# A fused attention and ternary-FFN kernel whose engine queues are written out in another order

## What is computed

```
h = concat(tok(x), txt)                                  # 16 x 165 x 256
h = h + attn(layernorm(h))
h = h + ffn(layernorm(h))

attn: q 16 heads, k and v 4 heads, head size 16, rotary embedding,
      scores masked to |i - j| <= 32, softmax, context, output projection
ffn:  act_quant(x) @ ternary(w1).T -> depthwise conv over 3 tokens + bias
      -> silu -> act_quant @ ternary(w2).T
act_quant: scale = 127 / max|row|, round, divide;  ternary(w): round(w / mean|w|) to -1, 0, 1
```

## Time and profile before

| | before |
|---|---|
| median of 3 runs | 406.79 us (406.76 to 406.89) |
| the profiled execution | 403.69 us |
| its span, first to last instruction | 401.9 us |
| PE busy | 343.6 us, 86% |
| DVE busy | 292.0 us, 73% |
| ACT busy | 258.2 us, 64% |
| POOL busy | 243.6 us, 61% |
| granted TensorE clock, mean share of full | 0.956 |

### The profile page before, as it was taken

How to read it: one execution, slowest core, us unless ns; L and a number is a source line. 1 busy time by engine, 2 the same in 40 slices (tenths; PEclk the granted TensorE clock), 3 DMA queues, 4 the chain that set the end, 5 groups by cost and what they waited for, 6 DMA issues and landing times.

```text
span 401.9 us, 8246 instructions
## 1 busy us (share of the span) xinstructions
PE 343.6 (86%) x2910; PEld 268.7 (67%) x2910; DVE 292.0 (73%) x629; ACT 258.2 (64%) x481; POOL 243.6 (61%) x240
## 2 busy tenths in 40 slices
PE   1588999899999999999999999999979989927435
PEld 1366667677777688868986788688758757716324
DVE  2256437943669888887789568889887988898961
ACT  3232455876768778877886778869667687626630
POOL 3418098099898993999699937983740661520500
PEclk9999899999999999999999999999999999977756
DMA  7682241000110100020002001100110100100011
GB/s 233 170 166 50 74 173 24 1 12 16 28 30 20 33 0 13 15 61 10 10 18 56 17 17 40 36 2 18 33 44 1 35 2 0 36 0 2 1 34 34
DMA packets 20228, 15.71 MB, mean 39 GB/s; under 512 B 11013, under 2 KB 19138, under 8 KB 20187
## 3 DMA queue, kind: packets, MB, share of 16 engines
q1 hardware_dynamic: 19292, 14.02, 13.5%
q10 hardware_dynamic: 895, 1.16, 1.1%
HBM read 7.91 MB, written 2.70 MB: 26 GB/s over the span
## 4 chain that ended last, share of the span: by engine, by line
PE 56%; DVE 14%; POOL 12%; ACT 6%; issue 5%; DMA 4%; SPq 1%; ACTq 0%; POOLq 0%; DVEq 0%
PE bank L1671 6%; PE bank L1763 5%; PE bank L1686 5%; PE bank L1591 4%; PE bank L1713 4%; PE bank L1739 4%; POOL shared L990 4%; PE bank L1643 3%; PE bank L1740 3%; PE bank L1662 3%; PE bank L1538 3%; PE bank L1654 2%; DMA cst<-in_consts 2%; PE bank L1704 2%; POOL shared L998 2%
## 5 line engine op out<-in xcount | busy, mean ns | idle before, releaser
L1333 DVE TENSOR_REDUCE mx<-bank 120x4 fp32r<-120x376 f32 (+3 forms) x88 | 44.6, 510 | 39.4 <-PE bank L1654 38.8
L1110 ACT COPY pT<-bank 94x480 f32<-94x480 f32 (+3 forms) x88 | 48.6, 556 | 18.9 <-PE bank L1671 17.5
L1671 PE MATMUL bank<-cst,pr 120*94 120x120 f32 (+3 forms) x352 | 50.6, 268 | 2.0 <-ACT pr L1101 1.8
L1101 ACT ACTIVATE pr<-bank 120x376 f32<-120x376 f32 (+3 forms) x88 | 39.8, 456 | 18.6 <-PE bank L1662 18.0
L1739 PE MATMUL bank<-xT_hi,w1T 128*128 128x330 f32 x128 | 45.5, 361 | 3.3 <-DVE xT_lo L1401 1.8
L1671 PEld LDWEIGHTS bank<-cst,pr 120*94 120x94 f32 (+3 forms) x352 | 36.8, 121 | 9.0 <-ACT pr L1101 4.4
L1740 PE MATMUL bank<-xT_lo,w1T 128*128 128x330 f32 x128 | 40.4, 320 | 0.0
L1763 PE MATMUL bank<-w2T,shared 128*110 128x256 bf16 x192 | 29.8, 309 | 9.6 <-ACT shared L1168 7.7
L1643 PE MATMUL bank<-kbd,q_hl 128*120 128x376 f32 (+3 forms) x88 | 34.5, 392 | 2.8 <-ACT pT L1110 2.3
L1662 PE MATMUL bank<-mx,neg_id 120*120 120x376 f32 (+3 forms) x88 | 34.2, 394 | 2.8 <-DVE mx L1333 2.7
L1654 PE MATMUL bank<-kbd,q_hl 128*120 128x376 f32 (+3 forms) x88 | 36.1, 411 | 0.0
(11 more groups left out here) (134 smaller groups left out, 901.5 us busy)
## 6 DMA issues: line engine op xcount, KB each, us to landing
out<-h SPq DMA_DIRECT2D x8, 330.0 KB
wn<-in_w SPq DMA_DIRECT2D x2, 1024.0 KB, 6.8
kbd<-kT SPq DMA_DIRECT2D x96, 20.6 KB, 1.9
shared<-in_x SPq DMA_DIRECT2D x4, 432.0 KB
h<-in_txt SPq DMA_DIRECT2D x1, 770.0 KB
...
```

The costliest lines, as they stand in the source:

```text
L1110: nc.scalar.copy(pT[0:cnt, g % 3, :], S_BANKS[g % 2][0:cnt, 0:HKV * QP]).then_inc(p_kept, 1)
L1333: nc.vector.tensor_reduce(mx[:, g % 4, :].bitcast(F32R), S_BANKS[g % 2][0:QP, 0:HKV * KEYS[j][1]].rearrange("p (k c) -> p k c", k=HKV), ax ...
L1671: o = nc.tensor.transpose(S_BANKS[g % 2][0:cnt, kv * QP:(kv + 1) * QP], pr[:, g % 3, kv * cnt:(kv + 1) * cnt], ident[0:QP, 0:QP])
```

## The change

The numbers of ORDER and ONCE change; no operation, buffer or wait does. On PE the same 624 operations come in another order, most of them moved by one to six places. A piece of the diff (three of its tables):

```diff
     'pe.scores': (
...
-        (373, 375, 385, 390, 399, 411, 420, 424, 429, 437, 439),
-        (447, 451, 465, 469, 479, 480, 489, 494, 499, 507, 510),
+        (373, 376, 384, 389, 400, 411, 413, 424, 428, 435, 438),
+        (446, 453, 459, 468, 478, 483, 487, 493, 499, 507, 513),
...
     'sp.place_k': (
-        (None,), (None,), (7,), (10,), (13,), (16,), (19,), (22,),
+        (None,), (None,), (8,), (10,), (12,), (14,), (18,), (22,),
     ),
...
     'sp.store': (
-        (12,), (15,), (18,), (21,), (23,), (24,), (25,), (26,),
+        (15,), (16,), (19,), (21,), (23,), (24,), (25,), (26,),
     ),
```

More of the change, by code:

```diff
@@ L129 @@
         (3, 4),
[L130 to L136, removed]
+        (19, 21),
+        (78, 80),
+        (126, 129),
+        (179, 182),
+        (248, 251),
+        (328, 334),
+        (396, 401),
     ),
@@ L139 @@
         (6, 7, 9),
[L140 to L146, removed]
+        (23, 30, 40),
+        (82, 86, 91),
+        (135, 143, 151),
+        (185, 190, 197),
+        (255, 262, 267),
+        (339, 343, 347),
+        (408, 417, 425),
     ),
@@ L149 @@
         (11, 12, 13),
[L150 to L156, removed]
+        (47, 57, 67),
+        (99, 108, 120),
+        (158, 169, 173),
+        (214, 223, 235),
+        (289, 301, 313),
+        (359, 371, 386),
+        (441, 451, 475),
     ),
@@ L212 @@
[L212 to L216, removed]
+        (42, 65, 89),
+        (114, 136, 149),
+        (187, 210, 237),
+        (265, 288, 315),
+        (342, 364, 383),
+        (415, 442, 467),
+        (489, 511, 534),
+        (557, 583, 599),
     ),
     'pe.select': (
[L219 to L224, removed]
@@ L225 @@
-        (495, 517, 538),
-        (564, 589, 601),
+        (48, 71, 92),
+        (121, 140, 157),
+        (191, 221, 239),
+        (270, 293, 322),
+        (344, 368, 388),
+        (422, 457, 471),
+        (495, 514, 543),
+        (563, 588, 601),
     ),
     'pe.out_proj': (
[L229 to L236, removed]
+        (51, 75, 95),
@@ L237 @@
+        (127, 145, 165),
+        (203, 227, 243),
+        (276, 296, 325),
+        (351, 380, 392),
+        (429, 462, 481),
+        (501, 516, 545),
+        (576, 591, 602),
     ),
     'pe.turn_xs': (
-        (146,), (203,), (286,), (389,), (438,), (511,), (571,), (603,),
+        (148,), (200,), (285,), (377,), (432,), (512,), (572,), (603,),
     ),
     'pe.up': (
[8 rows of a table removed]
[8 rows of a table added]
     ),
     'pe.turn_max': (
-        (206,), (276,), (353,), (442,), (502,), (565,), (610,), (617,),
+        (208,), (273,), (350,), (439,), (504,), (566,), (608,), (617,),
@@ L253 @@
     ),
     'pe.spread': (
-        (216,), (284,), (357,), (453,), (506,), (569,), (612,), (618,),
+        (217,), (283,), (356,), (450,), (509,), (569,), (611,), (618,),
     ),
     'pe.down': (
[L258 to L263, removed]
+        (234, 241, 252),
+        (304, 311, 332),
+        (382, 403, 418),
+        (472, 479, 490),
+        (519, 530, 538),
+        (579, 585, 592),
@@ L268 @@
         (6, 7),
[L269 to L272, removed]
+        (18, 20),
+        (54, 55),
+        (88, 89),
+        (126, 128),
         (175, 178),
-        (229, 232),
-        (274, 280),
+        (232, 235),
+        (276, 278),
     ),
     'act.keep_qk': (
[L278 to L285, removed]
+        (8, 10, 11),
+        (22, 30, 35),
+        (58, 61, 68),
+        (94, 99, 103),
+        (132, 136, 140),
+        (183, 187, 195),
+        (239, 242, 246),
+        (287, 292, 304),
     ),
     'act.keep_q': (
[L288 to L295, removed]
+        (14, 15, 16),
+        (39, 43, 49),
+        (72, 81, 83),
+        (111, 118, 122),
+        (151, 158, 166),
+        (204, 214, 221),
+        (256, 266, 269),
+        (309, 315, 338),
     ),
     'act.keep_k': (
-        (14, None),
-        (49, 51),
-        (85, None),
+        (17, None),
+        (50, 52),
+        (86, None),
         (124, None),
[L302 to L305, removed]
+        (171, None),
+        (228, None),
+        (273, None),
+        (348, None),
     ),
     'act.exp': (
[8 rows of a table removed]
[8 rows of a table added]
     ),
     'act.keep_p': (
[8 rows of a table removed]
[8 rows of a table added]
     ),
     'act.keep_ctx': (
-        (32, 45, 58),
-        (78, 92, 103),
-        (128, 147, 159),
+        (31, 45, 62),
+        (77, 91, 101),
+        (129, 146, 164),
         (186, 198, 217),
         (238, 253, 264),
-        (287, 306, 318),
-        (340, 354, 365),
+        (286, 307, 323),
+        (339, 352, 365),
         (385, 402, 414),
@@ L337 @@
     'act.keep_sel': (
[L338 to L345, removed]
+        (38, 51, 66),
+        (84, 96, 108),
+        (143, 155, 169),
+        (191, 205, 226),
+        (245, 260, 270),
+        (299, 319, 329),
+        (347, 358, 378),
+        (396, 408, 417),
     ),
     'act.quant_x': (
-        (93,), (134,), (189,), (248,), (288,), (350,), (391,), (None,),
+        (93,), (135,), (189,), (248,), (289,), (350,), (391,), (None,),
     ),
     'act.high_x': (
-        (100,), (144,), (200,), (271,), (307,), (357,), (397,), (420,),
+        (102,), (144,), (200,), (267,), (306,), (356,), (397,), (420,),
     ),
     'act.mid': (
[8 rows of a table removed]
[8 rows of a table added]
     ),
@@ L365 @@
         (167, 181),
-        (219, 236),
+        (218, 236),
         (284, 297),
-        (327, 342),
-        (373, 383),
+        (324, 341),
+        (372, 383),
         (410, 419),
@@ L373 @@
     'act.conv_g': (
-        (156, 160),
-        (204, 208),
+        (157, 159),
+        (202, 208),
         (254, 261),
-        (322, 326),
-        (355, 358),
+        (322, 327),
+        (357, 359),
         (398, 399),
-        (431, 432),
+        (430, 432),
         (436, 437),
@@ L397 @@
         (20, 29, 39),
-        (48, 54, 61),
+        (47, 54, 58),
         (79, 90, 101),
-        (119, 128, 142),
-        (154, 165, 172),
-        (189, 203, 216),
-        (227, 241, 252),
+        (118, 128, 142),
+        (155, 165, 171),
+        (189, 202, 214),
+        (228, 239, 252),
         (266, 282, 290),
@@ L435 @@
     'dve.silu': (
-        (71, 80),
+        (70, 80),
         (None, 114),
@@ L471 @@
     'dve.add_ffn': (
-        (102, 112, 115),
-        (136, 143, 156),
-        (171, 182, 188),
-        (218, 224, 229),
-        (243, 251, 256),
-        (278, 284, 286),
+        (103, 107, 115),
+        (136, 145, 156),
+        (175, 183, 191),
+        (218, 222, 230),
+        (244, 251, 256),
+        (278, 285, 287),
         (313, 316, 318),
```

99 lines of the change are left out of this document (48 added, 51 removed), and 154 rows, old and new, of the table ORDER.

## The result

| | before | after |
|---|---|---|
| median | 405.58 us of 20 runs (403.67 to 407.84) | 408.35 us of 20 runs (404.75 to 412.26) |
| ratio after to before, 95% interval | | 1.0053, 1.0028 to 1.0077 |
| the profiled execution | 403.69 us | 404.76 us |
| its span | 401.9 us | 403.0 us |
| PE busy | 343.6 us | 342.7 us |

The changed kernel is slower by 0.53%, about 2.1 us. The medians of the table differ by 2.8 us; they include two slow runs of the changed kernel (411.44 and 412.26 us), which the ratio leaves out. Forecast were 407.9 us and "slower by 0.2% to 0.7%". Sign and size came out; the sum that led there did not, as the trace shows at once.

A forecast was written before the change was run, and what follows sets the result against it. PE's own work bounds the kernel from 48 to 353 us, so reordering wins at most 16 us of idle time. Terms 1.7 + 0.2 - 0.8 - 0.4 - 0.4 + 0.4 + 0.4 = +1.1 us; median 407.9 us, range 404.4 to 411.2.

The forecast's parts named there:

- The forecast case: Whole kernel slower by 0.2% to 0.7%, likeliest 407.6 to 409.6 us; chance 0.33.
- start: 0 to 48 us: 0; if the cover is gone, one DVE copy of about 1 us is paid.
- pair 0: 48 to 80 us: +0.2 us, as turn_k(1,0) loses its 0.6 us of cover, for +0.4.
- single hops: 80 to 285 us: hops with under 0.6 us of PE work between their ends go from 5 to 13; +1.7 us.
- turn_xs(4): PE's 0.83 us wait near 255 us goes because POOL runs dequant_x(4) before rope(7,0); -0.8 us.
- place_k(5): DMA issue ahead of scores(5,0) ends about 4 us earlier with the store behind it, removing a 0.40 us wait; -0.4 us.
- turn_max(4) and scores(7,0): From out_proj(5,2): 1.2 us less standing still, but turn_k(7) moves 2.8 us of work back; -0.4 us, bounds -1.2 and +1.6.
- pairs 6 and 7: 305 to 353 us: +0.4 us for two out_proj of pair 6; other short hops hidden ahead of turn_xs(6).
- tail: Behind 353 us: mid(7,7) splits conv_g(6) on ACT, its second half ends 0.5 us later and delays down(6,0); +0.4 us.
- the two chains: The chains into turn_xs(4), -0.8 us, and through place_k(5), -0.4 us, both expected to lose their PE waits.
- The rival "clearly slower": DVE or ACT take an unready operation ahead of one PE needs; two such cases give +4.9, 411.7 us; chance 0.10.
- The clock: Rival: one more clock fall like that of 40 to 50 us costs 1.7 us, 409.6 us; chance 0.04.

The follow-up runs named there:

- run 7: Changed kernel with context(2,10) seven places earlier on PE and max_x(4) two places earlier on DVE; 400.57 us, 0.9891 of the kernel before.
- run 1: The changed kernel measured again with no edit; 409.18 us, 1.009 of the kernel before.
- run 5: Changed kernel with context(2,10) on PE seven places earlier, directly behind context(2,9); 406.26 us, 1.0018 of the kernel before.
- run 6: Changed kernel with max_x(4) on DVE two places earlier, ahead of add_ffn(2,1) and the taps of block 4; 402.50 us, 0.993 of the kernel before.
- run 10: Order of the kernel before up to about 240 us, changed order behind it, max_x(4) ahead of silu(3,0); 401.68 us, 0.9889 of the kernel before.
- run 3: Changed kernel with five tiny DVE tensor_scalar operations rewritten as scalar_tensor_tensor; 409.76 us, 1.0097 of the kernel before.
- run 2: Changed kernel with the maximum of scores(5,5) ahead of max_x(4) on DVE; 406.78 us, 1.0037 of the kernel before.
- run 11: Changed order with context(2,10) moved up until about 240 us, order of before behind it, max_x(4) ahead of silu(3,0); 404.58 us, 0.9988 of the kernel before.
- run 9: Kernel before with two DVE neighbours swapped, the taps of block 4 ahead of max_x(4); 412.90 us, 1.0168 of the kernel before.
- run 8: Kernel before with context(2,10) on PE six places later; 407.76 us, 1.0051 of the kernel before.

## Why the prediction was right, and where its steps were wrong

The forecast case, slower by 0.2% to 0.7%, came true by luck: two waits that are no terms of its sum made up for terms that were too high. The 407.9 us were luck as well, for the three runs that they start from had a median 1.2 us above that of the twenty, and the change was sized too small. By its own test, "a wait over 1.5 us on PE before 353 us that no line above names", the sum is refuted. Run 7 has neither wait, so its trace shows what the sum was meant to price. From cut to cut, the mended kernel (run 7) less the kernel before:

| step | predicted | measured, run 7 |
|---|---|---|
| start | 0 | within the 3.9 us scatter |
| pair 0 (first scores to out_proj(0,2)) | +0.2 | +0.1 |
| single hops, turn_xs(4), place_k(5) (89 to 269 us) | +1.7 - 0.8 - 0.4 | -1.2 |
| turn_max(4) and scores(7,0) (269 to 311 us) | -0.4 | -0.9 |
| pairs 6 and 7 (311 to 353 us) | +0.4 | -1.2 |
| tail | +0.4 | -0.5 (within 0.1 of 0 in runs 1, 5, 6 and 10) |
| sum | +1.1 | -3.7 |
| meeting of max_x(4) with silu(3,0) | not in it | +5.3 to +6.4 (first trace, runs 1, 3 and 5) |
| load_v(4) | not in it | +0.3 to +3.6 (first trace, runs 1, 2, 3 and 6) |

- *Single hops and the two chains, +0.5: the stops came, and the stretch is shorter all the same.* turn_xs(4) and scores(5,0) have no wait now, and in the first trace place_k(5) is issued at 207.24 instead of 212.94 and dequant_x(4) starts at 248.89 instead of 257.77, as predicted. In run 7 scores(5,8) waits 0.64 us, the stop that the sum named; shift(5,8) waits 0.87 instead of 0.48, shift(4,8) 0.55, and turn_xs(1), for which the sum had no term, 1.29 us for POOL. In exchange those of turn_xn(4,1), shift(2,6) and project(5,2), 0.36 to 0.57 us each, are gone. PE stands still 5.2 us between these cuts, and 4.6 in the kernel before. That is 0.7 us more before rounding, near the +0.5. What failed is the premise "the sum of work on each engine stays; only waits can change": PE's busy time is 173.1 us here and 175.0 before, with the clock full in both. Where one context stands directly behind another, it adds 0.21 us; elsewhere it adds 0.37. One alone in the trace of before, then two in a row in that of run 7:

```profile
220.99 0.44 PE L1686 MATMUL bank<-pT,vw 94*32 94x120 f32 x8
...
218.88 0.65 PE L1686 MATMUL bank<-pT,vw 78*32 78x120 f32 x16
```

Between these cuts there are 20 contexts behind a context in the new order and 13 before. The seven more come to 1.1 of the 1.9 us. This is read from the traces, and no run tested it.
- *turn_max(4), -0.4: sized too small.* Its wait went from 1.88 to 0.42 us, and scores(7,0) has none. The sum priced the wait by a trace in which the clock stayed full behind it; in the four traces named under run 11 the same wait brought 1.0 to 1.4 us more. The +2.8 us that I held back as a bound for turn_k(7) did not come. scores(6,6) and scores(6,7) wait 0.64 us each, and I had counted them as free; the piece is shorter all the same.
- *Pairs 6 and 7, +0.4: wrong sign.* In the trace of before scores(7,7) waits 0.64 us, and two more stops stand ahead of it:

```profile
321.50 0.43 PE L1643 MATMUL bank<-kbd,q_hl 128*120 128x376 f32 x1 [0.73 <-ACT pT L1110]
...
324.22 0.61 PE L1671 MATMUL bank<-cst,pr 120*78 120x120 f32 x4 [0.67 <-ACT pr L1101]
```

These are scores(7,5) and turn_p(7,4). In the new order all three are 0.2 us or less, and shift(7,5), turn_p(7,6) and spread(5) wait 0.5 us each. I had counted only what loses cover in the queue, not the waits in the trace that vanish.
- *Tail, +0.4: about 0.* conv_g(6) comes in two pieces as foreseen, and in run 7 down(6,0) waits 3.59 us instead of 3.33, but the end isn't later for it.
- *The rival "clearly slower"* had the right mechanism, a DVE or ACT operation in front of one that PE needs, at 1.88 us each and a chance of 0.10. Two such waits came, one per engine: 3.77 us on DVE, 1.96 on ACT. What I missed is that max_x(4) was ready; it was held while it ran. This is the first step that failed: "DVE's and ACT's queues were shifted along with PE's" was taken as a reason against such a wait, and the sum gave it nothing. I had quoted the shared port pair, and applied it only to POOL's operations, as half longer or shorter, never to a DVE operation of 0.17 us beside a POOL instruction of 3 us.
- *The clock*, priced apart at 1.7 us with a chance of 0.04, belongs to the long waits. It fell at the wait of 3.77 us each time, and the piece was longer by 1.6 to 2.6 us than the wait explains; the larger figure also holds 0.9 us before turn_max(3). Behind waits of 1.9 us it fell in runs 1 and 3 but not in run 6, and behind turn_max(4)'s 1.88 us in four traces of five.

So the change consists of a better order, worth 3.7 us in the trace of run 7, and two accidents that cost more. Between the first scores and the last out_proj run 7 gains 3.1 us, 1.8 by standing still less and 1.4 by a shorter busy time (both rounded). That both accidents are causes is shown by taking them out (runs 5, 6, 7), and for the first also by putting it into the other kernel (run 9); run 8 was to do that for the second and did not. Why the load lands 1.28 us after its last issue in one execution and 2.95 in another stays open.

In medians the kernel before is further behind run 10 (3.8 us) than in the traces (2.1 us). Most of that goes with the clock. The profiled execution, with a mean granted clock of 0.956, was one of the best. Of 72 executions of the kernel before in the three comparisons (one of 449.87 us left out), 12 had a clock of 0.952 or more and took 403.4 us in the median; the other 60 had 0.949 or less and took 405.5. The slow stretch behind turn_max(4) is one fall that the profiled execution lacked; that it is the usual one is likely from the four traces, but not shown for the executions without a trace. A better order gives that back too, so 3.7 us is its worth against the kernel before at its best.
